# The feed-forward weights' maximum over partitions taken by transposes in the drain, and the cross weights split among the first pair's jobs

## The reference

```python
x = x + attn(layernorm(x), Wq, bq, ...)      # (windowed + compressed + top-64) / 3
x = x + xattn(layernorm(x), ctx, ctx, mask)  # 16 heads of 64
x = x + ffn(layernorm(x), w1, b1, w2, b2)

def quant_per_tensor(x):
    scale = max(max(abs(x)), 1e-6) / 127
    return round(x / scale), scale
def qlinear(x, w, b):
    xq, sx = quant_per_tensor(x)
    wq, sw = quant_per_tensor(w)             # sw needs the maximum over all of w
    return (xq @ wq.T + b) * (sw * sx)
def ffn(x, w1, b1, w2, b2):
    return qlinear(gelu(qlinear(x, w1, b1)), w2, b2)
```

## Time and profile before

| | us |
|---|---|
| median of 3 runs | 1793.79 (1792.17 to 1795.85) |
| the profiled execution's own time | 1805.32 |
| its span | 1803.1 |
| mean granted clock of PE, share of full | 0.964 |
| busy: PE, DVE, ACT, POOL | 1601.0, 1517.7, 1059.2, 1055.4 |
| idle of POOL around the weights' `PARTITION_ALL_REDUCE` | 5.77 before it, 6.71 behind it |

### The profile page before, as it was taken

The page is one execution under the profiler, slowest core; times in us unless marked ns, Lnnn a source line. Parts: engine busy times, 40 slices in busy tenths (PEclk is TensorE's granted clock), DMA queues, the critical chain, the costliest instruction groups (busy, mean ns, idle before and its releaser), DMA issues.

```text
span 1803.1 us, 52021 instructions
## 1 busy us (share of the span) xinstructions
PE 1601.0 (89%) x16033; PEld 1421.2 (79%) x16052; DVE 1517.7 (84%) x6181; ACT 1059.2 (59%) x2205; POOL 1055.4 (59%) x1172
## 2 busy tenths in 40 slices
PE   5599999999999999999999999999999999768898
PEld 4488888888888888888888888888888888654465
DVE  3698888888898888888888888888888888539876
ACT  3455565565565555555555565556655565449875
POOL 2376666676666666666666666666676666631000
PEclk9799999999999999999999999999999999879999
DMA  6000000000000000000000000000000000212055
GB/s 196 1 19 23 21 26 26 26 26 26 26 26 26 25 26 26 26 19 20 23 26 26 26 26 26 25 18 26 26 26 26 26 26 21 83 53 77 31 169 175
DMA packets 77732, 71.01 MB, mean 39 GB/s; under 512 B 6272, under 2 KB 77184, under 8 KB 77696
## 3 DMA queue, kind: packets, MB, share of 16 engines
q1 hardware_dynamic: 76736, 70.41, 12.1%
q10 hardware_dynamic: 960, 0.13, 0.1%
HBM read 45.36 MB, written 25.17 MB: 39 GB/s over the span
## 4 chain that ended last, share of the span: by engine, by line
PE 43%; DVE 20%; issue 16%; ACT 9%; POOL 5%; DMA 5%; SPq 1%; DVEq 0%; ACTq 0%; POOLq 0%
PE banks L107 11%; PE banks L109 10%; PE banks L108 10%; DMA x_in<-in_x_dram 4%; DVE xn L1089 3%; PE banks L770 2%; DVE sparse_in L1201 2%; PE banks L660 2%; DVE stats L1079 2%; PE banks L794 2%; DVE scores L1122 2%; PE banks L1664 1%; PE banks L755 1%; ACT sparse_in L915 1%; DVE tile_max L1769 1%
## 5 line engine op out<-in xcount | busy, mean ns | idle before, releaser
L555 POOL TENSOR_TENSOR exp_t<-exp_copy,exp_t 128x512 f16<-128x512 f32 x256 | 299.2, 1174 | 198.1 <-ACT exp_copy L954 197.2
L549 POOL TENSOR_TENSOR shifted<-scores,score_max 128x512 f32<-128x512 f32 x256 | 267.4, 1049 | 49.6 <-DVE score_max L1122 35.4
L1122 DVE CUSTOM_DVE_ANT_0 scores<-banks,mask 128x128 f32<-128x128 f32 x1024 | 231.8, 285 | 12.3 <-POOL shifted L549 2.6
L541 POOL TENSOR_TENSOR v_nat<-kv_copy,v_nat 128x512 f16<-128x512 f32 x128 | 145.2, 1134 | 95.6 <-ACT kv_copy L942 95.5
L952 ACT ACTIVATE exp_t<-banks 128x512 f16<-128x512 f32 x256 | 152.8, 597 | 73.4 <-PE banks L770 69.8
L939 ACT ACTIVATE q_t<-banks 128x512 f16<-128x512 f32 x128 | 72.9, 596 | 194.4 <-PE banks L109 193.7
L107 PE MATMUL banks<-ctx_t,cross_Wk 128*128 128x256 f32 x512 | 154.0, 301 | 5.9 <-POOL cross_Wo L260 5.8
L942 ACT ACTIVATE kv_copy<-banks 128x512 f32<-128x512 f32 x256 | 155.3, 607 | 4.8 <-POOL k_t L541 4.8
L770 PE MATMUL banks<-ident,shifted 128*128 128x128 f32 x1024 | 155.7, 281 | 0.2 <-POOL shifted L549 0.2
L541 POOL TENSOR_TENSOR k_t<-kv_copy,k_t 128x512 f16<-128x512 f32 x128 | 148.5, 1169 | 10.8 <-issue 6.7
L954 ACT ACTIVATE exp_copy<-banks 128x512 f32<-128x512 f32 x256 | 154.5, 604 | 0.0
(11 more groups left out here) (242 smaller groups left out, 5693.8 us busy)
## 6 DMA issues: line engine op xcount, KB each, us to landing
x_in<-in_x_dram SPq DMA_DIRECT2D x32, 256.0 KB, 2.8
ctx_in<-in_ctx_dram SPq DMA_DIRECT2D x32, 256.0 KB, 2.7
x_residual<-x SPq DMA_DIRECT2D x64, 128.0 KB, 1.7
x_normalised<-normed SPq DMA_DIRECT2D x32, 256.0 KB, 2.2
shared<-x_normalised SPq DMA_DIRECT2D x8, 1024.0 KB, 5.2
shared<-x_residual SPq DMA_DIRECT2D x16, 512.0 KB, 3.8
out_dram<-shared SPq DMA_DIRECT2D x16, 512.0 KB, 2.9
mask<-in_fside_Bx1xSxS_dram SPq DMA_DIRECT2D x64, 64.0 KB, 1.9
```

The costliest lines, as they stand in the source:

```text
L541: pool.tensor_tensor(hilo(dst, *at)[LO], src, hilo(dst, *at)[HI], ALU.subtract).then_inc(kv_split, 1)
L549: pool.tensor_tensor(shifted[:, q % 2], scores[:, q % 2], score_max[:, q % 2, :].unsqueeze(2).to_broadcast([P, QUAD, P]), ALU.subtract).th ...
L555: pool.tensor_tensor(exp_t[:, q % 2, LO], exp_copy[:, q % 2], exp_t[:, q % 2, HI], ALU.subtract).then_inc(exp_split, 1)
L1122: op = dve.tensor_tensor_reduce(scores[:, q % 2, h, :], sc_bank(q)[:, tile(h)], mask[:, b, :], 1.0, NEG, ALU.add, ALU.max, score_max[:, q ...
```

## The change

It has seven parts, all in the start, the drain and the feed-forward.

- `weight_peaks` moves on DVE from `body(-1)` to the drain, behind `add_mask(7)`. `weight_all` on POOL goes. The maximum over partitions is now taken by two transposes in the drain: PE turns the 128x2 of `wabs` into 2x128 (`weight_row`), DVE takes the maximum along it (`weight_one`), and PE spreads the two numbers over all partitions (`weight_spread`).
- `quantise(0)` moves on DVE behind `heads_lo(3)`, `quantise(1)` behind `x2_statistics`. All eight `ffn_weights` move on PE behind `output(1)`, all eight `weight_take` on ACT behind `normalise_x2`.
- `largest(0)` and `largest(1)` go from POOL. `peak_spread` does the same work by transposes on PE. The first stands behind the eight `ffn_weights`, the second behind the second product of the feed-forward's second pass.
- The jobs of the cross weights 4 to 7 move into `body(-1)` (PE ahead of `raw_scores`, ACT behind `J_V1`). PE's one wait for all 16 becomes a wait for the four jobs of the weight that is used, ahead of its use in `body(0)`.
- `cross_copy` has four slots where it had two.
- The bias products (`fold_biases`, `fold_biases_lo`) move behind `x_transpose(0)` on PE and behind `lo(J_X)` on DVE. DVE takes the statistics of pair 0 ahead of the weights' copies, and normalises ahead of `fold_lo`. POOL's `add_output_bias(0)` moves between jobs 7 and 8 of `cross_lo`.
- Waits that repeat another are left out or moved: `evacuated` waits only for a job in the other bank. In the loop this leaves one wait fewer ahead of `attend` and puts one for bank 1 ahead of the second of `queries`.

The diff, cut to its core:

```diff
-    cross_copy = sb("cw_copy", [P, 2, 512])
+    cross_copy = sb("cw_copy", [P, COPIES, 512])           # COPIES = 4
-    N_T, N_A, N_VO, N_COL, N_ROW, N_CROSS = 0, 3, 4, 5, 6, 7
-    bank_of = lambda n: psum[:, PREP_BANK + n % 4, :]
+    N_T, N_A, N_VO, N_COL, N_ROW, CROSS = 0, 3, 4, 5, 6, 100
+    TURNS = [0, 1, 2, N_A, N_VO, *range(CROSS, CROSS + 4), N_COL, N_ROW, *range(CROSS + 4, CROSS + 16)]
+    bank_of = lambda n: psum[:, PREP_BANK + TURNS.index(n) % 4, :]
...
-    def wait_cross(pe):
-        pe.wait_ge(cross_split, len(cross_jobs))
+    def wait_cross(pe, n):
+        pe.wait_ge(cross_split, 4 * ("Wk", "Wv", "Wq", "Wo").index(n) + 4)
...
-            if k >= 2:
-                act.wait_ge(cross_split, k - 1)
+            if k >= COPIES:
+                act.wait_ge(cross_split, k - COPIES + 1)
...
         weights_of["constants"](pool)
         body(-1, False, False, True)
-        weights_of["cross_lo"](pool)
-        ffn_of["weight_all"](pool)
+        weights_of["cross_lo"](pool, 0, 8)
+        add_output_bias(0)
+        weights_of["cross_lo"](pool, 8, 16)
...
-            if ahead and not front:
-                ffn_of["weight_peaks"](dve)
             if back:
                 heads_lo(3, i - 1)
+            if back and not front:
+                ffn_of["quantise"](dve, 0)
...
+    def weight_row(pe):
+        pe.wait_ge(abs_ready, 2)
+        pe.transpose(psum[0:2, W_BANK, 0:P], keep["wabs"][:], keep["ident"][:]).then_inc(abs_row, 1)
+    def weight_one(dve):
+        dve.wait_ge(abs_row, 1)
+        dve.tensor_reduce(keep["wmax"][0:2, 0:1], psum[0:2, W_BANK, 0:P], AX, ALU.max).then_inc(abs_one, 1)
+    def weight_spread(pe):
+        pe.wait_ge(abs_one, 1)
+        pe.transpose(psum[:, W_BANK, P:P + 2], keep["wmax"][0:2, 0:1].to_broadcast([2, P]),
+                     keep["ident"][0:2, 0:2]).then_inc(abs_all, 1)
+    def peak_spread(pe, k):
+        bank = PEAK_BANK[k]
+        pe.wait_ge(peak_own, k + 1)
+        pe.transpose(psum[0:1, bank, 0:P], peak[:, 2 * k:2 * k + 1], keep["ident"][:]).then_inc(peak_row, 1)
+        pe.wait_ge(peak_one, k + 1)
+        pe.transpose(psum[:, bank, P:P + 1], peak[0:1, 2 * k + 1:2 * k + 2].to_broadcast([1, P]),
+                     keep["ident"][0:1, 0:1]).then_inc(peak_all, 1)
...
-        largest(0)
         pool.wait_ge(scales_done, 1)
         round_x(1)
...
     def tensor(pe):
+        peak_spread(pe, 0)
         pe.wait_ge(w_taken, W_JOBS)
...
             dve.tensor_reduce(peak[:, 2 * k:2 * k + 1], maxima, AX, ALU.max).then_inc(peak_own, 1)
+            dve.wait_ge(peak_row, k + 1)
+            dve.tensor_reduce(peak[0:1, 2 * k + 1:2 * k + 2], psum[0:1, PEAK_BANK[k], 0:P], AX, ALU.max).then_inc(peak_one, 1)
             dve.wait_ge(peak_all, k + 1)
```

208 lines of the change are left out of this document (112 added, 96 removed).

## The result

The changed kernel took 1784.21 us (median of 10 runs, 1777.72 to 1796.81), the kernel before 1796.62 on the same chips (10 runs, 1792.17 to 1802.16). The ratio is 0.9938 with a 95% interval of 0.9913 to 0.9964: 12.4 us, or 0.6%, faster. The prediction was 1783.6 in a range of 1777 to 1788. The profiled execution took 1782.82 us with a span of 1781.0, so it is 22.1 us shorter than the one read before (span 1803.1), which is more than the medians differ. Where those 22 us lie is the first thing to find.

What follows compares the result with a forecast made beforehand. Steady pairs, PE 92% busy, fill 1490 of 1803.1 us; gains were sought in start, drain and feed-forward. Start -12.2, drain +2.2, feed-forward -0.9 and +0.7 sum to -10.2 us, carried to the 1793.79 median: 1783.6, range 1777 to 1788.

Steps and rivals of the forecast that it cites:

- Step 1: Start, PE: transposes ahead of the bias products bring the first product with xn to 28.8, 3.5 us earlier.
- Step 2: Start, POOL: cross weights and `x_bias` end at 50.0 instead of 55.5 and no longer hold PE.
- Four slots take nothing off: Start: four copy slots don't shorten POOL's end; they let ACT's last copy end near 45.5, not 53.7.
- Step 3: Start: `self_softmax` waits for DVE alone, 50.6 to 52.8; `wabs`, 4.47 us, is gone; `probs` at 54.7.
- Step 4: Start: PT0 at 54.7, PT1 at 56.5, K2 2.65; pair 1's x transposed at 59.5, not 71.75: -12.2 us.
- Rivals B and D: Start: B, half its gain hidden, about 1787.8, chance 0.15; D, start does nothing, 1793.8, chance 0.03.
- The collision: Drain: DVE's `quantise(1)` beside POOL's small operations puts `shift` 4.25 us behind the moments, not 1.9; `normed` gains 0.3.
- turn-taking: Drain: DVE and POOL alternate, one whole instruction at a time, from `var_eps` to `shift`.
- The drain's net to the scale: Drain: weight jobs, then transposes and maximum, make the scale at 1607.1 against 1604.85: +2.2 us.
- -0.9 and +0.7: Feed-forward: POOL's rounding on time saves 0.9 us at its start; transposes replacing the middle reduction cost 0.7.
- rival A: Drain gives nothing back: PE stays at its high level or DVE and POOL don't collide; 1779.3, chance 0.25.
- Rival C: Pairs' loop: the new bank 1 wait stalls PE, slower; at 0.5 us a round 1798.6, chance 0.03.

Runs made afterwards that it cites:

- e3: Changed kernel, but each first use of the cross weights waits for all sixteen parts; pair 1's x at 58.86 us (changed kernel 57.35), not timed as a ratio.
- e2: Changed kernel with two copy slots for the cross weights instead of four; 0.9929 of the kernel before.
- e4: Changed kernel with DVE's maxima over the weights back at the start, behind `sparse`; last three stages 243.48 us against 241.52.
- e8: Kernel before with its three POOL reductions replaced by transposes, cross weights' jobs, slots and waits unchanged; 0.9925 of the kernel before.
- e10: Changed kernel's start with the old drain order and transposes for later maxima, but POOL's weight reduction at the start again; 0.9912 of the kernel before.
- e6: Changed kernel with DVE's rounding of the second weight moved behind the maximum of x2; last three stages 244.16 us against 241.52.
- e1: Changed kernel with its last maximum, in the middle of the feed-forward, by POOL's reduction again; last three stages 241.22 us against 241.52.
- e11: Fastest kernel tried (drain's weight work moved into waits), but with the maximum of x2 by POOL's reduction; last three stages 240.94 us against 234.67.

## Why the prediction was right, and where its terms were off

The time was right to 0.6 us, and that close it was by luck. The change itself was forecast as -10.2 and measured as -12.4, while the reference median came out 2.8 higher than in the runs shown, and the two nearly cancel. The mechanisms of the start and of the drain were right in the main; terms of the sum were off by up to two microseconds.

**Step 1**, PE's order: the first xn product 3.5 us earlier was forecast, 6.9 came. PE began 1.8 earlier with `ident`, a gain that the prediction does not have at all; the folds were 0.6 shorter by the clock; and `Wk`'s 16 transposes took 2.1 us and not 2.79, at granted clock 1.00. **Step 2**, POOL done at 50.0 and no longer on the path: done at 47.6, and e3 shows that it is off the path. "Four slots take nothing off" was wrong by 1.3 us or more (e2). **Step 3**, DVE sets the time: `self_softmax` for 50.6 to 52.8, measured 47.68 to 49.94, so 2.26 for 2.2 and 2.9 earlier, with the first product's 3.4. `mix` to the end of `probs` was 2.85 for 1.9 (49.97 to 52.82), since one pair of its operations took 1.50 beside POOL's `k_t`. The 4.47 us of `wabs` were worth 1.1 (e4). **Step 4**, PT1 1.8 behind PT0, then 2.65: measured 1.91 and 2.69. The term, -12.2, measured -14.4 at pair 1's x and -14.15 at the first `normed`. The 2.2 more are the first product's: most of them is `ident`, a mechanism that the prediction did not have, and the rest a size. e8 and e10 put the mechanism itself at 6.8 us for POOL's reduction, in either order. Rivals B and D fall.

**The drain.** Output(0) 1.3 earlier (1.0 forecast), output(1) 3.15 (2.5). `quantise(0)` was hidden, as said. The collision came: `shift` ends 3.5 us behind the moments' end and not 4.25, because `rstd` waited for both of DVE's operations and `scaled_mean` for none, where I had them alternate. So `normed` came 1.5 us earlier and not 0.3. The Trainium skill, page "SBUF — State Buffer", section "Who interferes with whom", says that DVE and GpSimd hold their shared port pair as an exclusive lock for a whole instruction. The trace agrees: `rstd`, issued at 1573.87, ends at 1576.23, 0.03 behind DVE's second operation; with DVE's work moved away it took 0.72 (e6). But that second operation started at 1574.97, behind `rstd`, and still went first; the prediction's turn-taking was its own reading. Six weight jobs took 5.56 us, forecast 5.7, and the scale was 8.01 behind `normed`, forecast 8.7. Two transposes and a maximum cost 0.9 from `peak_row` to the scale, forecast 1.2. The drain's net to the scale was +0.35, forecast +2.2.

**The feed-forward.** Up to the second layer's scale it was -0.20, as the sum had it (-0.9 and +0.7): -0.59 up to `peak`, with POOL's rounding on time and the granted clock at 0.74 and not 0.50 behind the scale, and +0.39 in the middle (0.94 for 0.55). From the second scale to the end, where nothing is changed and nothing was forecast, came the other -2.1, and 1.7 of it is the clock's step there. So the three stages, -1.9 together, don't decide for rival A, "the drain gives nothing back": forecast +2.0, rival A -2.3, and without the step the profile has -0.2, halfway between. With the start the stages give -16.05, or -14.35 without the step, which would be 1780.6 or 1782.3 from 1796.6; the median says 1784.2. The rounds scatter by more than that.

Rival C, a stall in the pairs by the new bank waits, falls: 47.20 us a round against 47.16, and no kind of round is longer than with the old loop.

The Trainium skill, page "GPSIMD Engine Reference", section "Instruction dispatch", has approximately 6 us for the first call of a freshly loaded kernel. The runs show 5.77, 5.82, 5.83 and 5.85, counted from the end of POOL's instruction before and not from the operand. So the wait for `peak` in the middle, 38.9 us, covers it (0.55 in e1), and the 2.2 us of the start (e10) and of the drain (e11) do not.

## What to carry to other kernels

Look for what POOL's reduction over the partitions costs behind it as well as ahead of it: 5.8 us before and 6.7 to 7.8 after, and free only where POOL has been idle for that long. Two transposes and a small maximum cost 0.9 us, if PE isn't full at that place. And when a change moves filler work (rounding, weight transposes) along with it, test the move apart from the rest: here the idea was worth 6.8 us at the start, and the filler's new places lost 3.4 to the old ones and 6.85 to better ones. Before a difference of a microsecond or two is put down to an edit, compare the granted clock stage by stage: in four of the runs above 1.7 us of the difference are the clock's.

## What the runs showed of the hardware that was not expected

- `ident`'s mask, POOL's first operation of its kind, stands at 1.2 to 1.4 us in eleven kernels and at 11.3 and 11.8 in the two that have a reduction over the partitions in the middle of the feed-forward. Reductions at the start (e10) or in the drain (e11) alone don't do it. In the two that reduction is POOL's last operation, in the eleven a rounding of x is. The traces have two `MODIFY_POOL_CONFIG` of POOL ahead of each reduction (48.54 and 48.57 in e10), two more right behind each that is followed by another kind of work (55.13 and 55.16), and two at the start of every execution, 1.08 to 1.37, ahead of the mask. So it may be that the return from the last reduction, which costs 6.7 to 7.8 us elsewhere, is paid by the next execution. No run tests it.
- The eight products of the first fold take 3.7 to 3.8 us in eight executions and 2.0 in five. Products 0.43 us apart in the eight, until the clock's record begins, and 0.22 behind that show that PE is at the low level until then; in the five the rise comes ahead of the fold. The view's 1.00 there is no reading. What sets its time was not found.
- Work that starts earlier on PE can end later: output(0) began 0.9 us earlier in e4, at granted clock 0.50 and not 1.00, and its result came 0.6 later.
- A round of the pairs takes 45.9, 46.8 or 47.8 us: 0.9 by whether DVE's `xn` or POOL's `exp_t` starts first, which goes with a landing some 0.1 us earlier or later, and 1.0 by a stretch at the low clock behind the longer wait. Only 69 of 377 rounds are short. If all were, the 29 would be some 40 us shorter (an estimate, 45.9 for their mean of 47.3), more than everything else in this study; an order in which `exp_t` can't come first is untested.
